# Expert stage: routing weights spread over the unit rows by transfers from DRAM, shared expert first, projection bias on GpSimd

## What is computed

```python
# both layers
x = x + ga * attention(h)              # attention ends in concat @ Wo + bo
# layer 0, feed-forward: 8 routed experts and a shared one, H = 176 hidden units each
scores = softmax(xf @ gate_w.T)
_, idx = top_k(scores + gate_b, 2)
rw = zeros((T, 8)).at[rows, idx].add(take(scores, idx))
h  = silu((xf @ w1 + b1) * (xf @ w3 + b3))          # [token, expert, unit]
oe = einsum('teh,ehd->ted', h, w2) + b2
y  = einsum('te,ted->td', rw, oe)
z  = silu((xf @ sw1 + sb1) * (xf @ sw3 + sb3)) @ sw2 + sb2
x  = x + gb * (y + z)
```

## Time and profile before

| | before |
|---|---|
| median of 3 runs | 1121.09 us (1120.15 to 1122.63) |
| profiled execution | 1120.04 us |
| its span, first to last instruction | 1118.3 us |
| busy, share of the span | PE 90%, DVE 71%, ACT 67%, POOL 46% |
| granted TensorE clock, mean | 0.96 |
| DMA | 51.59 MB, 46 GB/s over the span |

### The profile page before, as it was taken

The page is one execution under the profiler, slowest core; times in us unless marked ns, Lnnn a source line. Parts: engine busy times, 40 slices in busy tenths (PEclk is TensorE's granted clock), DMA queues, the critical chain, the costliest instruction groups (busy, mean ns, idle before and its releaser), DMA issues. The chain is left out here.

```text
span 1118.3 us, 23277 instructions
## 1 busy us (share of the span) xinstructions
PE 1008.5 (90%) x8884; PEld 557.4 (50%) x8884; DVE 798.2 (71%) x1352; ACT 754.8 (67%) x1381; POOL 513.9 (46%) x735
## 2 busy tenths in 40 slices
PE   4789999889897999999999969999989899999896
PEld 2233333333335888888888833333333333333574
DVE  2658777887753666766677578888897888896375
ACT  2368777877682655565555528889887788888663
POOL 4446665665431011011101336767767676755344
PEclk9599999999896999999999978999999999999999
DMA  6432221222102000000000211112021120200001
GB/s 187 148 117 80 70 55 49 68 75 65 52 23 60 1 1 1 1 1 1 1 2 1 57 58 58 42 40 69 15 77 30 51 62 21 73 9 23 23 29 48
DMA packets 47714, 51.59 MB, mean 46 GB/s; under 512 B 11745, under 2 KB 41066, under 8 KB 47090
## 3 DMA queue, kind: packets, MB, share of 16 engines
q1 hardware_dynamic: 47602, 50.09, 15.6%
HBM read 17.02 MB, written 2.64 MB: 18 GB/s over the span
## 5 line engine op out<-in xcount | busy, mean ns | idle before, releaser
L733 ACT ACTIVATE at_E<-at_Sb 128x512 f32<-128x512 f32 x832 | 445.4, 597 | 102.7 <-PE at_Sb L582 97.4
L803 DVE TENSOR_REDUCE at_mx<-at_Mb 128x2 f32<-128x1024 f32 x256 | 297.0, 1216 | 40.4 <-PE at_Mb L545 39.3
L630 PE MATMUL at_Ob<-at_E,VP 128*32 128x256 f32 (+2 forms) x2816 | 212.9, 376 | 14.9 <-ACT Oev L759 9.7
L582 PE MATMUL at_Sb<-QP,KP 64*128 64x512 bf16 (+3 forms) x1024 | 205.6, 347 | 13.1 <-ACT full_k L340 3.6
L912 POOL TENSOR_TENSOR at_E<-at_E,at_factor 128x512 f32<-128x512 f32 x128 | 162.6, 1273 | 93.0 <-ACT at_E L733 82.8
L545 PE MATMUL at_Mb<-KP,QP 62*128 62x512 bf16 (+3 forms) x1024 | 180.7, 359 | 23.5 <-DVE at_mx L803 20.4
L806 DVE TENSOR_REDUCE at_mx<-at_Mb 128x2 f32<-128x768 f32 (+1 forms) x128 | 138.2, 1087 | 61.5 <-PE at_Mb L545 60.4
L923 POOL TENSOR_SCALAR_AFFINE_SELECT at_E<-at_E 128x512 f32<-128x512 f32 x128 | 82.7, 659 | 87.6 <-ACT at_E L733 87.4
L1241 ACT ACTIVATE ex_th<-ex_z 128x512 f32<-128x512 f32 x104 | 65.7, 632 | 81.4 <-DVE ex_z L1304 79.9
L630 PEld LDWEIGHTS at_Ob<-at_E,VP 128*32 128x32 f32 x2816 | 57.1, 108 | 116.4 <-issue 93.7
L582 PEld LDWEIGHTS at_Sb<-QP,KP 64*128 64x128 bf16 x1024 | 75.3, 96 | 79.3 <-ACT at_E L733 38.4
(11 more groups left out here) (193 smaller groups left out, 1503.8 us busy)
## 6 DMA issues: line engine op xcount, KB each, us to landing
QP<-q SPq DMA_DIRECT2D x96, 128.0 KB, 2.4
KP<-k SPq DMA_DIRECT2D x96, 128.0 KB, 2.4
ctxN<-Oev SPq DMA_DIRECT2D x16, 256.0 KB, 2.9
denB<-rdram SPq DMA_DIRECT2D x64, 64.0 KB
gates<-gates_dram SPq DMA_DIRECT2D x1, 2048.0 KB, 7.3
QP<-at_nrow SPq DMA_DIRECT2D x128, 4.0 KB
out<-x SPq DMA_DIRECT2D x8, 256.0 KB, 2.3
w_raw<-in_w SPq DMA_DIRECT2D x2, 832.0 KB, 6.1
```

What stands on the lines that cost most here:

```text
L582: return pe.matmul(out[:, at:at + SEQ - q0], KP[p0:p0 + ROWS_H, b % 2, 2 * g + a, kt * P:(kt + 1) * P], QP[p0:p0 + ROWS_H, b % 2, 2 * g + ...
L630: last = pe.matmul(Ob[VW * i:VW * (i + 1), 0, q0:q1], weights_of(b, G, kt, i, q0), moving, start=(kt == 0 and q0 == 0), stop=False, skip_g ...
L733: nc.scalar.activation(dst, src, ACT.Exp).then_inc(s["s_read"], 1)
L803: v.tensor_reduce(mx[:, G % 2, :, t % 2, t // 2], src, AX.X, ALU.max).then_inc(s["m_read"], 1)
```

## The change

1. **Routing weights.** `selr`, `rwr`, `Rb`, the matmul into `Rb` and `split_rw` are gone, with the load and the copy of the selection matrix in attention 0. ACT copies the weights of a batch (`read_rw`) into rows 64 to 72 of a tile `hs`; SP writes 8 of these rows to DRAM (`send_weights`) and reads each expert's row back to the partitions of its units (`spread_weights`), into `R`, a ring of 8 tiles in SBUF. `hidden` reads `R` and waits for the slot's semaphore.
2. **Shared expert first.** Its 176 units are now tiles 0 and 1, the 8 routed ones tiles 2 to 12. For tiles 0 and 1 silu writes to `hs`, `hidden` is left out, and `down` follows silu.
3. **Output bias.** Tile 1 has 48 units of the shared expert. Its rows 64 to 72 hold the weights (the ninth is one), and `w2` has b2 there, so the four matmuls with `b2` are gone.
4. **Start of the expert phase.** No memset and no `split_rw` ahead. `finish_recip` stands at j = 1, `finish_context` at 4, `finish_project` at 6, `finish_add` at 7, with a bank `Fb` of its own. SP sends the weights of batch 0 at the end of attention 0 and spreads the first three tiles ahead of `finish_spread`.
5. **Projection bias.** `brow` is a tile of 128 rows, formed from `bopB`, which setup fills with two matmuls and a copy. GpSimd waits for it and adds it to x of the batch, 128 x 512. The matmul with the row of ones is gone.

```diff
@@ finish_weights (GpSimd)
     p.tensor_tensor(sb["wog"][:], sb[f"wo{layer}"], gate[:, b, :], ALU.mult).then_inc(s["wog"], 1)
-    p.tensor_tensor(sb["brow"][:], sb["bop"][:, layer, :], gate[0:1, b, :], ALU.mult).then_inc(s["wog"], 1)
+    p.tensor_tensor(sb["brow"][:], sb["bopB"][:, layer, :], gate[:, b, :], ALU.mult).then_inc(s["brow"], 1)
+    p.wait_ge(s["brow"], b + 1)
+    xb = sb["x"][:, b * SEQ:(b + 1) * SEQ].rearrange("p (t d) -> p t d", t=TILES)
+    p.tensor_tensor(xb, xb, both(sb["brow"][:], TILES), ALU.add).then_inc(s["wog"], 1)
@@ finish_project (TensorE)
-    return pe.matmul(bank, sb["ones"][:], sb["brow"][:].unsqueeze(1).to_broadcast([1, TILES, P]),
-                     start=False, stop=True, skip_group_check=True)
@@ attention 0, ScalarE and GpSimd
-                if causal and divmod(beat, BPB) == (7, 4):
-                    a.wait_ge(ex["sel"], 16)
-                    nc.scalar.activation(sb["selr"][:], sb["w_raw"]["w1"][0:R_LOW + ALL_EXP, :], ACT.Copy)
+                if causal and (n, at) == (6, 6):
+                    p.memset(sb["hs"][:, :, 1, :], 0.0).then_inc(ex["zero"], 1)
@@ expert_phase, SyncE
+            def send_weights(bn, half):
+                sp.wait_ge(s["rwT"], bn + 1)
+                if bn >= 2:
+                    sp.wait_ge(s["hh"], ROUTED * (bn - 1))
+                sp.dma_start(sb["rw_dram"][half], hs[RW_AT:RW_AT + EXPERTS, half, 1, :]).then_inc(s["rwd"], 16)
+            def spread_weights(bn, half, tiles):
+                sp.wait_ge(s["rwd"], 16 * (bn + 1))
+                for j in tiles:
+                    r = ROUTED * bn + j
+                    if r >= RING:
+                        sp.wait_ge(s["hh"], r - RING + 1)
+                    for e, p0, p1 in experts_of(j):
+                        sp.dma_start(R[p0:p1, r % RING, :], sb["rw_dram"][half, e:e + 1, :].partition_broadcast(p1 - p0))\
+                          .then_inc(sb["spread"][str(r % RING)], 16)
             finish_gather(sp, sb, at, last_b)
+            spread_weights(0, 0, range(3))
             finish_spread(sp, sb, at, last_b)
+            spread_weights(0, 0, range(3, RING))
@@ hidden (VectorE)
-                v.tensor_tensor(hh[:, q, :], Rb[:, q, :], th[:, q, :], ALU.mult).then_inc(s["hh"], 1)
+                v.wait_ge(sb["spread"][str(r % RING)], 16 * sends(r))
+                v.tensor_tensor(hh[:, r % 2, :], R[:, r % RING, :], th[:, r % 2, :], ALU.mult)\
+                 .then_inc(s["hh"], 1)
@@ up (TensorE)
-                pe.matmul(Rb[:, q, :], selr[:, cols], rwr[0:R_ROWS, half, :], start=True, stop=True)\
-                  .then_inc(s["up"], 1)
@@ down (TensorE)
-                    for t in range(TILES):
-                        pe.matmul(Yb[:, 0, t * P:(t + 1) * P], rwT[half][:, t * P:(t + 1) * P], sb["b2"][:],
-                                  start=(t == 0), stop=False, skip_group_check=True)
```

195 lines of the change are left out of this document (105 added, 90 removed).

## The result

The changed kernel takes **1075.56 us** in the median of 4 runs (1072.24 to 1079.09), beside 1120.62 us for the kernel before in 4 runs (1117.26 to 1122.63): a ratio of **0.960**, 95% interval 0.957 to 0.962. The forecast was 1074.6, range 1062 to 1090. The sum is right, but each of its four terms is off. In the profiled executions the steady batches of the experts gave 1.8 us less than forecast, their start 2.8 more, attention 0 3.6 less and attention 1 2.2 less; the spikes, put at 0, gave 0.8. In all that is 4.0 us less than forecast. That the median lies only 1.0 us from the forecast is in part luck: the executions of one kernel lie some microseconds apart, and the profiled one of the changed kernel, 1077.53, was 2.0 above its median.

What follows compares the result with a forecast made beforehand. PE was taken to bound the experts and, narrowly, the second attention. Steady batches 26.6, experts' start 12.5, attention 1 6.2 and attention 0 1.2 sum to 46.5 us gained: forecast 1074.6 us, range 1062 to 1090.

Steps and rivals of the forecast that it cites:

- the term for what is given back: Experts' steady batch: 0.24 us for PE waits at `ex_hh` plus 0.16 for POOL collisions, taken off the gain per batch.
- The 0.16 for collisions with POOL: Experts' steady batch: 0.16 us lost where `hidden`, now with both operands in SBUF, meets POOL instructions.
- the two tiles at half the clock: First batch of the experts: 12 matmuls each 0.23 us longer at half the clock, 2.8 us in all.
- The term for `denB`: First batch of the experts: DVE held at tile 4, PE waiting about 1 us; taken as 1.2, bounds 0 and 3.
- The transfers: Experts: one store and 18 spreads per batch on SP, costed at 0; bounds 0 and 16 us.
- Rivals 4 and 5: Experts: transfers are the bound, 1238 us, chance 0.03; or `hidden` waits for each batch's first spread, 1088.6 us, chance 0.08.
- The projection bias in attention 1: Second attention: removing 1.05 us of PE matmul in seven batches, 85% kept, gains 6.2 us; bounds 3 and 7.4.
- 7.8 lost, 3 recovered, 1.3 at the end: Attention 0: six PE waits for `at_nmx` lose 7.8 us, ACT and DVE catching up recovers 3, phase end loses 1.3.
- The 7.4 us for the matmuls: Attention 0: dropping the bias matmul saves PE 7 x 1.05 = 7.4 us.
- setup's additions against a dropped load: Setup's two matmuls and copy against a dropped load, with attention 0's dropped `selr` copy: 0, between 1 lost and 1.5 gained.
- Rival 1: Clock falls again in the experts' first batch (-5), GpSimd's addition costs its full wait in attention 0 (-5): 1084.5, chance 0.13.
- Rival 2: Experts: `hidden` and POOL collide on the shared SBUF port; half the worst gives 20 us back, 1095; chance 0.07.

Runs made afterwards that it cites:

- old-order run: Changed kernel with the last batch's context back at its old places in the first batch of the experts: 1091.13 us, 0.973 of the kernel before.
- bias on PE: Changed kernel with the projection bias again a one-row matmul on PE and no GpSimd addition to x: 1076.74 us, 0.966 of the kernel before.
- weights later: Changed kernel with PE's transposition of the routing weights at tile 11 instead of 10, ACT's copy behind that silu: 1072.62 us, 0.963 of before.
- doubled addition: Changed kernel with one more GpSimd 128 x 512 addition in each of attention 0's first six batches: 1087.42 us, 0.974 of the kernel before.
- moved addition: Changed kernel with GpSimd's addition to x 4 beats later in attention 0, 11 later in attention 1: 1061.37 us, 0.952 of the kernel before.

## Why the prediction held, and where it did not

**The tile and the batch: right.** 2.29 us a tile, 33.3 a batch, 4.26 us less work for PE. The seven batches gave 24.8 in place of 26.6, within the bounds 22 and 30. What was off is the term for what is given back: 0.4 us per batch counted, 0.9 measured. I had looked for late tiles at `ex_hh` alone. The transposition of the routing weights is another place where PE meets a chain on DVE that did not get shorter, and it is of the same kind as the earlier trace rows. The 0.16 for collisions with POOL was spent on something that costs 0.

**The start: right in kind, 2.8 us too small.** The gain was 15.3, forecast 12.5. The difference has the size of one term of the sum, the two tiles at half the clock, 2.8 us; the smaller terms are off by some tenths each and cancel. In neither profile of the changed kernel did the clock fall. With a longer pause it does, and the first two tiles then run at 0.50, as the term had it; but the batch then grows by 1.3 us and not by 2.8, since waits behind the second tile shrink. Where it fell without a longer pause, it cost 0.5 and 1.3 us. So the term was too large even where it applies. The term for `denB`, 1.2 us, came out as small waits (0.60 the longest that I read, at 351.84). The old-order run shows that the terms hang on the places of the context: 11.7 us, of which the prediction saw only the part that the trace of before could show.

**The transfers: right.** 0 us; with twice as many still 0 per steady batch. Rivals 4 and 5 fall: no PE wait for DMA, and the longest landing is 6.3 us, where the first spread of the third batch is issued at 409.36 and `hidden` reads it at 418.49, 9.1 us later.

**The projection bias in attention 1: right in kind, the size within its bounds.** Forecast 6.2, in the first pair of profiles 4.0, from 391.7 to 387.7. The short batches give 47.09 against 46.08, 7 us if all seven were short. The two profiles with one long batch each, the bias on PE and the weights later, differ by 389.7 - 384.0 = 5.7, but that pair was picked for its likeness: the mean of the three profiles with the matmul is 390.6 and that of the nine without it 386.3, a difference of 4.3. All of these lie within the bounds of 3 and 7.4. Whether long batches are more frequent without the matmul, 16 of 45 and 4 of 15 here, these few profiles can't tell.

**Attention 0: wrong sign, and two errors.** Forecast +1.2, measured -2.4, within the bounds of -5 and +6. The step that failed is the balance "7.8 lost, 3 recovered, 1.3 at the end": the edit costs 6.7 to 7.3 us there, the changed kernel's two profiles against that with the bias on PE. The wait itself was sized right, 1.35 us more. Nothing of it is recovered, as the doubled addition shows, and the clock takes about 1.1 us more behind it in most batches. The step said nothing of a clock in attention. Of the 14.2 us between the changed kernel and the moved addition, six waits at 1.35 are 8.1, the end of the phase is 1.4, about as forecast, and the 4.7 left go by this count to the clock. The 7.4 us for the matmuls was right: with the addition elsewhere 7.0 come out. Against this stands a gain that I had put at 0, "setup's additions against a dropped load". The load of 832 KB was worth 3.1 us by its place in SP's queue, and I had priced it by its bytes. Rival 1 was half right: attention 0 gives back, the start does not.

**The shared port.** In the changed kernel `hidden` takes 1.58 us in place of 0.69 when GpSimd has begun 0.24 us earlier an instruction of 1.27: it ends 0.55 us after it, as if it had begun just before GpSimd was done. And GpSimd's `ex_h_lo` takes 1.82 in place of 1.30 when `hidden` has begun just before it. Each waits for nearly all that is left of the other's instruction, 0.89 of 1.03 us and 0.52 of 0.66. The Trainium skill (SBUF — State Buffer, section "SBUF: two separate sides") calls the shared pair an exclusive lock; the trace agrees, more clearly than the 0.33 us of the earlier trace rows did. Rival 2 falls on its number: one meeting per batch in which `hidden` waits and not four, at a place with slack.

## What to carry to other kernels

Before an instruction is moved onto an idle engine, look at who stands behind it on that engine: with the same 1.27 us on GpSimd in all cases, its place decided between 7 us gained and 7 lost in one phase. When a transfer is taken out of a queue or put into it, price it by what stands right behind it and who waits for that, not by its bytes. And before comparing whole phases, read a gain per batch from batches that neither a late transfer nor a fall of the clock has lengthened: a clock of 1.00 alone is no proof, as eight long batches at 1.00 show here.
